# Rearranging the ramp of a deformable-attention kernel: halves of rows in the first norm, image 1's convolution spread over waits, query transfers held behind rows of maxima

## The reference, cut to what matters

```
x_ln   = layernorm(x, ln_g, ln_b)                   # over channels, 1024 rows an image
q      = x_flat @ wq + bq                           # x_flat is x_ln, reshaped
q_img  = q.reshape(b, c, h, w)
o      = gelu(depthwise_conv7x7_stride2(q_img) + dw_b)
offs   = conv1x1(o)                                 # two offsets a sample point
interp = grid_sample_bilinear_zeros(x, refs + tanh(offs))   # 256 samples an image
k = v  = interp @ wv + bv
qh     = heads(q @ mq_w + mq_b); kh = heads(k @ mk_w + mk_b); vh = heads(v @ mv_w + mv_b)
att    = softmax(qh @ kh^T) @ vh                    # 8 heads, 1024 x 256 scores each
z      = att @ mo_w + mo_b + x
out    = gelu(layernorm(z) @ mlp_w + mlp_b) + z
```

## Time and profile before

| | |
|---|---|
| median of three runs | 526.87 us |
| the profiled execution's own time | 524.93 us |
| its span | 523.1 us |
| PE busy | 456.5 us, 87% |
| DVE busy | 286.2 us, 55% |
| ACT busy | 211.7 us, 40% |
| mean granted PE clock | 0.964 |

### The profile page before, as it was taken

One profiled execution on the slowest core, in us unless ns is written; L12 is line 12 of the kernel. 1 busy time (PEld: TensorE's weight loads), 2 busy tenths in 40 slices (PEclk: granted clock), 3 DMA queues, 4 the chain that ended last, 5 costly groups with the idle time before them and its releaser, 6 DMA issues.

```text
span 523.1 us, 9272 instructions
## 1 busy us (share of the span) xinstructions
PE 456.5 (87%) x3727; PEld 320.2 (61%) x3727; DVE 286.2 (55%) x609; ACT 211.7 (40%) x336; POOL 120.6 (23%) x163
## 2 busy tenths in 40 slices
PE   0978988978599999998999999989989897988966
PEld 0956755645357666665687676656766574665734
DVE  3619433855555437847863375457546737537253
ACT  1112110555134333675416145655346474463340
POOL 5601200176001200375102000681012021100000
PEclk9998888999798999999999999999989998899989
DMA  7492885785804790157026920293117310000112
GB/s 209 92 207 43 187 127 104 127 197 70 117 0 59 101 235 7 59 90 111 9 82 101 184 34 2 82 121 63 43 42 102 62 42 1 2 3 1 41 41 82
DMA packets 30489, 42.90 MB, mean 82 GB/s; under 512 B 6075, under 2 KB 21230, under 8 KB 30446
## 3 DMA queue, kind: packets, MB, share of 16 engines
q1 hardware_dynamic: 23886, 35.08, 37.0%
q0 software_dynamic: 3584, 4.50, 3.2%
q10 hardware_dynamic: 2976, 2.73, 2.7%
HBM read 16.16 MB, written 4.19 MB: 39 GB/s over the span
## 4 chain that ended last, share of the span: by engine, by line
PE 64%; DVE 11%; DMA 8%; POOL 5%; issue 5%; ACT 5%; SPq 0%; ACTq 0%; DVEq 0%; POOLq 0%
PE ps_d L735 8%; PE ps_d L723 5%; PE ps_d L860 5%; PE ps_d L755 5%; PE ps_d L837 5%; PE ps_d L937 5%; PE ps_s L784 4%; PE ps_v L826 4%; PE ps_t L803 4%; PE ps_v L820 4%; DMA q_st<-mx_t 3%; PE ps_d L879 2%; DMA xa<-in_x_dram 2%; DVE mx L1560 2%; POOL samp L1871 2%
## 5 line engine op out<-in xcount | busy, mean ns | idle before, releaser
L1189 ACT ACTIVATE prob<-ps_t 128x1024 f32<-128x1024 f32 x64 | 65.4, 1022 | 102.3 <-PE ps_t L803 101.4
L1560 DVE TENSOR_REDUCE mx<-ps_s 128x4 f32<-128x1024 f32 x64 | 78.2, 1222 | 34.4 <-PE ps_s L784 33.3
L1843 POOL DMA_DIRECT2D q_st<-mx_t x64 | 34.1, 534 | 261.2 <-ACT mx_t L1181 244.8
L735 PE MATMUL ps_d<-cstack,conv_w 128*32 128x256 f32 x1024 | 59.9, 388 | 3.5 <-DMA cstack<-qpad 3.1
L784 PE MATMUL ps_s<-k_st,q_st 96*128 96x256 f32 x256 | 51.4, 325 | 8.5 <-DVE mx L1560 5.6
L803 PE MATMUL ps_t<-q_st,k_st 98*128 98x256 f32 x256 | 43.9, 295 | 12.7 <-DMA q_st<-mx_t 6.1
L735 PEld LDWEIGHTS ps_d<-cstack,conv_w 128*32 128x32 f32 x1024 | 35.7, 110 | 25.3 <-issue 6.2
L784 PEld LDWEIGHTS ps_s<-k_st,q_st 96*128 96x128 f32 x256 | 37.3, 198 | 21.7 <-DVE mx L1560 9.6
L803 PEld LDWEIGHTS ps_t<-q_st,k_st 98*128 98x128 f32 x256 | 36.7, 198 | 15.4 <-issue 7.7
L820 PE MATMUL ps_v<-prob,vh 128*32 128x256 f32 x512 | 36.2, 402 | 0.8 <-DVE att L1574 0.7
L1574 DVE TENSOR_TENSOR att<-ps_v,rden 128x256 f32<-128x256 f32 x32 | 13.6, 424 | 40.3 <-ACT rden L1200 40.2
(11 more groups left out here) (177 smaller groups left out, 751.0 us busy)
## 6 DMA issues: line engine op xcount, KB each, us to landing
q_st<-q_parts SPq DMA_DIRECT2D x42, 256.0 KB, 6.8
xa<-in_x_dram SPq DMA_DIRECT2D x8, 512.0 KB, 9.0
z_all<-in_x_dram SPq DMA_DIRECT2D x8, 512.0 KB, 9.2
out_dram<-z_all SPq DMA_DIRECT2D x8, 512.0 KB, 2.6
cstack<-qpad SPq DMA_DIRECT2D x22, 180.5 KB, 5.7
k_st<-cstack SPq DMA_DIRECT2D x24, 128.0 KB, 3.9
q_st<-z_all SPq DMA_DIRECT2D x6, 256.0 KB, 5.6
cstack<-att SPq DMA_DIRECT2D x6, 180.5 KB, 6.0
```

Of the source, the lines that this page charges most:

```text
L735: ins = pe.matmul(ps[32 * k:32 * k + 32, 0, :], conv_w[:, cb * 4 + k, y, x, :], cstack[:, cb, k, y:y + HG_, x:x + WG_], start=n == 0, stop ...
L1189: drain(act.activation(prob[:, u % 2, 2 * pr:2 * pr + 2].rearrange("p h m s -> p (h m) s"), ps_t[:], ACT.Exp), t_ring, "t", b, u, pr)
L1560: drain(dve.tensor_reduce(mx[:, u % 2, half, :], ps_s[:], AX.X, ALU.max), s_ring, "s", b, u, half)
```

## The change

It does six things.

1. **Norm by halves.** Statistics, deviation, scale and shift of image 0 are done for the first four row tiles and then for the last four, and `q_image` goes by row half across both channel blocks instead of block by block. `keep_clock` issues 8 transposes for 16.
2. **Queries and biases in waits.** The query part of the fused bias and `queries(0, 0, [0])` move ahead of image 0's convolution; the key part moves between the convolution and its offsets; `queries(0, 1)` moves ahead of `keys(0)`.
3. **Query image of image 1.** Its second block leaves slot (0, 0): half of it now stands ahead of `keys(0)` and half behind.
4. **Image 1's first convolution block** was 6 and 10 of its 16 steps in slot (0, 1). Now steps 0 to 5 come before slot (0, 0), 6 to 9 in it, 10 to 12 and 13 to 15 in slot (0, 1).
5. **Key transfers.** Two of the six `k_st` parts of image 0 are issued by ACT and not by SP.
6. **Query transfers.** `stack_q(0, 1)` is split by head group: group 0 behind the row of maxima of unit 1 as before, group 1 behind that of unit 2. `load_z(0)` waits for the row of unit 3, and `stack_q(1, 0)` for the row of unit 5.

```diff
+STEPS_OF_1 = range(6), range(6, 10), range(10, 13), range(13, TAPS * TAPS)
...
 def dense_order():
-    order = [("qimg", 0, cb, jp) for cb in range(CB) for jp in range(2)]
-    order += [("conv", 0, cb) for cb in range(CB)] + [("off", 0), ("qh", 0, 0, 0)]
-    order += [("qimg", 1, 1, jp) for jp in range(2)] + [("qh", 0, 0, 1), ("kh", 0)] + [("qh", 0, 1, hg) for hg in range(NHG)]
+    order = [("qimg", 0, cb, jp) for jp in range(2) for cb in range(CB)]
+    order += [("qh", 0, 0, 0)] + [("conv", 0, cb) for cb in range(CB)] + [("off", 0), ("qh", 0, 0, 1)]
+    order += [("qimg", 1, 1, jp) for jp in range(2)] + [("qh", 0, 1, hg) for hg in range(NHG)]
+    order += [("qimg", 1, 0, 0), ("kh", 0), ("qimg", 1, 0, 1), ("conv", 1, conv_halves(1)[0])]
...
@@ SP: stack_k @@
+                        if b == 0 and row == 1:
+                            continue
...
@@ SP: slot @@
+                if b == 0:
+                    if s == 2:
+                        behind_max_row(b, 2)
+                        stack_q(b, 1, [1])
+                    if s == 3:
+                        behind_max_row(b, 3)
+                        load_z(b)
+                    if s == 5:
+                        behind_max_row(b, 5)
-                if s == 2 and cur and b < B - 1:
+                if s == 2 and 1 <= b < B - 1:
                     load_z(b)
...
@@ SP: ramp @@
             stack_q(0, 0, [0])
+            stack_q(0, 0, [1])
             stack_conv(1, 1)
             stack_k(0)
-            stack_q(0, 0, [1])
             stack_conv(1, 0)
             behind_max_row(0, 0)
             load_a(2)
             behind_max_row(0, 1)
-            stack_q(0, 1)
+            stack_q(0, 1, [0])
...
@@ PE: keep_clock @@
-                for _ in range(4):
+                for _ in range(2):
...
@@ PE: slot @@
                 if s == 0 and b == 0:
                     value_rows(b)
-                    q_image(n, 0)
...
                 if in_front(b, s, "conv0"):
-                    conv(n, conv_halves(n)[0], FIRST_STEPS if b == 0 else range(TAPS * TAPS))
+                    conv(n, conv_halves(n)[0], STEPS_OF_1[2] if b == 0 else range(TAPS * TAPS))
...
+                if s == 0 and b == 0:
+                    conv(n, conv_halves(n)[0], STEPS_OF_1[1])
...
                 if in_front(b, s, "conv0") and b == 0:
-                    conv(n, conv_halves(n)[0], LAST_STEPS)
+                    conv(n, conv_halves(n)[0], STEPS_OF_1[3])
...
@@ ACT @@
             act.wait_ge(setup_pool, P_EPS)
-            row_deviation(0)
+            row_deviation(0, [0])
             setup_queries()
...
             setup_weights()
+            act.wait_ge(setup_dve, D_QUERY_BIAS)
+            query_hi(0, 0, [0])
             row_deviation(1)
...
             key_hi(0)
-            query_hi(0, 1)
+            for hg in range(NHG):
+                act.wait_ge(k_hi_done.sem, k_hi_done.at(0, hg + 1))
+                act.dma_start(k_st[32:64, 0, :, hg, :].bitcast(F32), k_parts[:, 0, hg, :].bitcast(F32)
+                              ).then_inc(k_in[hg].sem, 16)
...
@@ DVE: ramp @@
-            row_stats(0)
+            half_stats(0, first)
+            row_moments(0, first)
+            half_stats(0, second)
             for_norm.wait(dve)
-            row_norm(0, range(NJ))
-            row_norm(0, range(NJ, NT))
-            setup_orders()
+            row_norm(0, first)
+            row_moments(0, second)
+            row_norm(0, second)
...
-            q_image(0, 0)
-            q_image(0, 1)
+            q_image(0, 0, [0])
+            q_image(0, 1, [0])
+            setup_orders()
+            q_image(0, 0, [1])
+            q_image(0, 1, [1])
+            setup_columns()
+            setup_query_bias()
```

More of the change, by code:

```diff
@@ L136, in dense_order @@
         if b == 0 and s == 0:
-            order += [("vh", b)] + [("qimg", n, 0, jp) for jp in range(2)]
+            order += [("vh", b)]
         if in_front(b, s, "off"):
@@ L1120, in with_gelu, with row_deviation @@
                 tables[0] = "gelu"
-            def row_deviation(b):
+            def row_deviation(b, halves=range(2)):
                 with_exp()
-                act.wait_ge(ln1_aggr.sem, ln1_aggr.at(b, NT))
-                act.activation(rs1[:], mv1[:, :, 1], ACT.Ln, bias=eps[:]).then_inc(ln1_log.sem, 1)
-                act.wait_ge(ln1_log.sem, ln1_log.at(b, 1))
-                act.activation(rs1[:], rs1[:], ACT.Exp, scale=-0.5).then_inc(ln1_dev.sem, 1)
+                first, end = halves[0], halves[-1] + 1
+                rows = slice(first * NJ, end * NJ)
+                act.wait_ge(ln1_aggr.sem, ln1_aggr.at(b, end * NJ))
+                act.activation(rs1[:, rows], mv1[:, rows, 1], ACT.Ln, bias=eps[:]).then_inc(ln1_log.sem, end - first)
+                act.wait_ge(ln1_log.sem, ln1_log.at(b, end))
+                act.activation(rs1[:, rows], rs1[:, rows], ACT.Exp, scale=-0.5).then_inc(ln1_dev.sem, end - first)
             def residual_deviation(b, cb):
@@ L1161, in query_hi @@
                     last = [(q_in[1][hg], b - 1) for hg in range(NHG)] if b else []
-                for hg in range(NHG):
+                for hg in groups:
                     if last:
```

143 lines of the change are left out of this document (81 added, 62 removed).

## The result

Over 21 runs of each kernel the changed one takes 520.02 us in the median (516.67 to 524.84), the kernel before 524.35 (522.23 to 529.97): ratio 0.9905, 95% interval 0.9880 to 0.9931. That is 4.3 us between the medians, 5.0 by the ratio, where the prediction had 16.5, and the time lies 1 us above the range of 503.5 to 519. The profiled run of the changed kernel took 518.39 us (span 516.5), that of before 524.93 (span 523.1): 6.6 us less.

What follows compares the result with a forecast made beforehand. PE, busy 87% of the span, was taken as the bound; terms 0 + 4.65 + 5.3 + 1.4 + 5.2 = 16.5 us took the profiled 524.93 to 508.4, predicted as 509.5 us, range 503.5 to 519.

Steps and rivals of the forecast that it cites:

- First norm and keep-clock, -0.5 us at the first convolution: Start of image 0: norm by halves and eight fewer transposes make the first convolution start and end 0.5 us late.
- Queries and query bias into the wait, +3.3 us behind the offsets: Before the first convolution: bias and queries fit PE's 3.1 us wait, so queries behind the offsets start 3.3 us earlier.
- to the keys: 0: From queries behind the offsets to image 0's keys: keys start at the old time, 64.7 us; ends +1.5 and -1.6.
- Key transfers: 0: From keys to first scores: ACT issuing two of six parts changes nothing; 7.3 us stay.
- Slot (0, 0): +4.65: Slot (0, 0): scores, full-rate value rows and four convolution steps take 5.0 us instead of 9.65.
- slot (0, 1): +5.3: Slot (0, 1): six convolution steps left instead of 16, so 6.3 us instead of 11.6, with row 0 landing in time.
- Slots (0, 2) to (0, 4): +1.4: Slots (0, 2) to (0, 4): the 2.4 us "issue" wait goes, less 1.0 for DVE work ahead of maxima.
- Slot (0, 7): +5.2: Slot (0, 7): without the 6.1 us row wait, queries start 6.2 us earlier, less a bill of 1.0 for late-landing queries.
- query traffic isn't what delays the rows: Rival, 0.07: the 6.1 and 2.4 us row waits stay or move to unit 6's row; 9 us go, 518.
- The waits move to the queries: Rival, 0.08: queries behind row 5 land late, stopping ACT and DVE; the slot (0, 7) gain goes, 513.
- The ramp gives back its part: Rival, 0.15: keys no earlier, clock falls near 72 us, row 0 late; slots (0, 0) and (0, 1) keep 3 us, 516.
- slower: Rival, 0.04: without the eight transposes PE stays at half rate through query image and fused weights; 530.

Runs made afterwards that it cites:

- e1: The changed kernel with the two setup_orders copies back ahead of the query-image additions, as in the kernel before; 517.81 us, 0.9851 of the kernel before.
- e11: The changed kernel with POOL's conv_w products made to wait for DVE's two setup_orders copies, which keep their new place; 516.20 us, 0.9842 of the kernel before.
- e4: The changed kernel with the old SP order of the query transfers; 529.45 us, 1.0091 of the kernel before.
- e6: e1 with image 1's first query transfers no longer held behind row 5 of the maxima; 521.19 us, 0.9900 of the kernel before.
- e5: e1 with both query groups of unit (0, 0) computed ahead of image 0's convolution; 517.78 us, 0.9863 of the kernel before.
- e7: e1 with all query parts of unit (0, 1) sent behind row 1 of the maxima, not half behind row 2; 521.98 us, 0.9952 of the kernel before.
- e8: e1 with 16 keep-clock transposes again; 516.52 us, 0.9846 of the kernel before.
- e9: e1 with SP holding image 1's first planes until image 0's gather of corners has landed; 515.08 us, 0.9816 of the kernel before.
- e10: e8 with SP holding image 1's first planes until image 0's gather of corners has landed; 516.55 us, 0.9846 of the kernel before.
- e12: e10 with both query groups of unit (0, 0) ahead of image 0's convolution, as in e5; 513.71 us, 0.9790 of the kernel before.
- e2: e1 with all six key transfers of image 0 issued by SP again, in the old order; 517.64 us, 0.9871 of the kernel before.
- e3: The kernel before with only the new SP order of query transfers; 522.13 us, 0.9933 of the kernel before.

## Why the prediction was wrong

- **"First norm and keep-clock, -0.5 us at the first convolution": the step that failed.** It measured -4.3 us. I counted what the order puts ahead of the second row half on PE and DVE, and not `setup_orders`, which the same diff moves between the halves; its 0.43 us would have been nothing, but behind POOL's product it is 4.56. e1 and e11 take it away in two ways and get the convolution to 30.11 and 29.46. It is 3.8 of the 9.9 us between forecast and profile. The half-rate bill of 0.8 us came out in this profile (8.56 us for the 32 passes, 7.74 before); as e4 took 7.34 and e6 8.79 with the same 8 transposes, that was luck in part.
- **"Queries and query bias into the wait, +3.3 us behind the offsets" and "to the keys: 0".** The bias and queries did leave the place behind the offsets: the next queries start 0.9 us behind the offsets' start, not 3.8, a gain of 2.9. But keys came 18.75 us behind it (50.40), against 17.30 before and 18.0 forecast: in part the clock, which fell again as I had allowed for, in part 1.3 us of waiting for samples. I had estimated samples and PE to tie at 63 and gave that no price. The runs show the tie: whenever PE was faster (e4, e5, e7, e8, e11), it waited 4.9 to 5.7 us for samples. The gather it waited for had image 1's planes beside it (e9, e10 and e12 take 1.7 to 2.7 us off by moving them) and the query parts as well. e1 and e11 win back 2.8 and 3.3 us by their ratios, of 4.2 and 4.8 us at the convolution; e11's longer wait for samples (5.7 us) shows where some of that went.
- **"Key transfers: 0".** Scores come 8.36 us behind the keys, not 7.47: -0.9. Why stays open: e2, with SP issuing all six, took 7.52, but so did e3, and it took 8.46.
- **"Slot (0, 0): +4.65" and "slot (0, 1): +5.3".** Measured +4.9 and +5.0. Right in mechanism and size: value rows at full rate, six steps instead of sixteen, row 0 in time.
- **"Slots (0, 2) to (0, 4): +1.4".** The "issue" wait is gone, yet the profiled run lost 1.4 us, so the term is off by 2.8. Slot (0, 4) took 12.1 us there and 8.9 in e1, e2, e3, e9, e10, e11 and e12. In the longer ones ACT has a wait of 2.1 to 2.8 us that the profile gives to no engine of the core:

```profile
107.87 1.02 ACT L1219 ACTIVATE prob<-ps_t 128x1024 f32<-128x1024 f32 x1 [2.80 <-remote]
```

  It is also in e5, e6 and e8 (slots of 9.9 to 13.3 us), and absent where the slot takes 8.9. What it is stays open; with e1's 24.9 us for the three slots, against 26.7 before, the term is +1.8.
- **"Slot (0, 7): +5.2".** The 6.1 us wait went as forecast, and e6 brings it back. To the queries it gave 4.7 and not 6.2, PE waiting 2.7 us for maxima; the landing of the queries and the `zn` wait took 0.8, near the 1.0 forecast. So the term measured 3.9. The landing at 141.83 (I had 143) is two errors that cancel: the parts were sent from 127.5 and not from 131, and took 14.4 us and not 12. The bill of 1.0 fits this profile only: with the hold, the stretch from queries to turned rows is 13.8 to 16.6 us over all kernels, and 13.0 in the three without it, a bill of 0.8 to 3.6.
- **Of the rivals,** "query traffic isn't what delays the rows" has fallen: in e6 and e7 a row behind six query parts makes PE wait 6.0 and 3.5 us, and in e1, behind none or three, 1.2 at most. The Trainium skill's rule of turns between queue rows (DMA: Bandwidth & Descriptors, Queues, rings and completion order) would let a 4 KB transfer of POOL pass SP's backlog. These waits disagree with it, and so does the gather of e12, which moves nothing until 54 us beside a full SP queue. "The waits move to the queries" came true in part, with the bill just named. "The ramp gives back its part", with 516, was nearest to the time, with a mechanism that did not occur: rows landed in time and slots (0, 0) and (0, 1) kept their 10 us. The loss was made earlier. A late first convolution was only in my "slower" rival, and there by the clock.
- **The range.** Its inner ends of 505 and 515 are counted from 508.4, the profiled execution, and not from the predicted 509.5, and no term stands behind the 1.5 us from 505 down to 503.5.

## What to carry to other kernels

When a diff moves work on one engine, list everything in the moved block and look at what the engine that shares its ports is doing there: a copy of 0.4 us can be 4.6. When a stretch ends in a tie between PE and a gather, making PE faster is worth nothing, and may be worth less if PE's results send transfers into the gather; try holding those, and count what they delay in their turn. A transfer taken out of a stretch may still be queued ahead of it: look at what the queues move there, and not only at what is issued there. Two edits that each look like a gain have to be timed alone as well: here one of them alone was slower than before.

## What the runs showed of the hardware

The clock behind the offsets is not set by PE's program alone. e1 and e9 have the same PE instructions and start the offsets at 46.33 and 46.28; the windows of 48 to 50 us, e1 and then e9, read:

```profile
48.00:50.00 2.00, 2.00 (x3) 0.68 (x2) 1.58 (x10) 0.00 (x0) 0.02 (x1) 0.50 0.05 5
```

```profile
48.00:50.00 2.00, 2.00 (x8) 1.31 (x7) 1.57 (x11) 0.69 (x1) 0.07 (x1) 1.00 0.12 17
```

One run was at 1.2 GHz there, the other at 2.4. e6 and e7, with the same PE instructions too, split the same way (0.69 and 1.00). PE was ready for the keys at 63.8 and 62.1 (their starts less the waits for samples), so it is worth 1.7 us, as much as some of the edits; single profiles can't tell those. Where PE then stood 5 us for samples (e4, e5, e7, e8, e11), the granted clock fell to 0.50 late in the wait or right behind it; so it did behind the 2.0 us of e12, but not behind the 2.3 us of e2 or the 1.3 and 1.7 us of e10 and e9. Of the four profiles whose clock was at 0.50 behind the offsets in the new order (the changed kernel, e1, e2, e6), none had PE idle over 0.61 us from the start of the convolution on, so the prediction's hope that a filled wait keeps the clock high did not hold.

A copy on DVE that takes 0.25 us alone ends only with POOL's product when it comes while one runs: 0.93 and 3.71 us in the changed kernel, 2.04 and 3.71 in e4. And what POOL issues behind a backlog of SP can wait for it: no packet of the gather moves in e12 from 50.89 to 54 us, and a 4 KB row takes 9.7 us behind six query parts in e6. Where SP's parts came behind the first list (e9), both queues moved, from 53 us on, with shares that changed from one microsecond to the next.
